# A gated delta-rule layer with a mixture of experts: reciprocal deviations reach all partitions through DRAM instead of through TensorE

## The reference

```python
def step(S, t):
    q_t, k_t, v_t, a_t, b_t = t
    y = einsum('bhvk,bhk->bhv', S, k_t)
    err = y - v_t
    S = a_t[..., None] * S - (b_t[..., None] * err)[..., None] * k_t[:, :, None, :]
    o = einsum('bhvk,bhk->bhv', S, q_t)
    return (S, o)
...
mu = mean(o, axis=-1, keepdims=True)          # over the 128 channels of a head
var = mean(square(o - mu), axis=-1, keepdims=True)
o = (o - mu) * rsqrt(var + LN_EPS) * ln_g + ln_b
o = (o * sigmoid(x @ Wg).reshape(b, t, H, D)).reshape(b, t, H * D)
return o @ Wo
```

## Time and profile before

| what | value |
|---|---|
| median of 3 runs | 3097.45 us (3096.15 to 3103.75) |
| span of the profiled execution | 3102.6 us |
| PE busy | 2732.2 us (88%) |
| DVE busy | 2239.8 us (72%) |
| ACT busy | 1610.3 us (52%) |
| POOL busy | 1377.8 us (44%) |
| granted TensorE clock, mean | 0.976 of full speed |
| DMA queue of SP | 258.51 MB, 31.5% of 16 engines' span |

### The profile page before, as it was taken

One profiled execution on the slowest core, in us unless ns is written; L12 is line 12 of the kernel. 1 busy time (PEld: TensorE's weight loads), 2 busy tenths in 40 slices (PEclk: granted clock), 3 DMA queues, 4 the chain that ended last, 5 costly groups with the idle time before them and its releaser, 6 DMA issues. The chain is left out here.

```text
span 3102.6 us, 48417 instructions
## 1 busy us (share of the span) xinstructions
PE 2732.2 (88%) x14144; PEld 1863.5 (60%) x14144; DVE 2239.8 (72%) x4680; ACT 1610.3 (52%) x3516; POOL 1377.8 (44%) x1760
## 2 busy tenths in 40 slices
PE   7999999768898888988889888898888888859999
PEld 3555555446666666666666666666666666635555
DVE  6777777677888878888788887888887888623332
ACT  6666666545555555555555555555555555412111
POOL 3666676734544445444454444544445444310000
PEclk9999999989999999999999999999999999979999
DMA  3655556533232232322323223232223222034120
GB/s 124 241 225 206 233 230 239 196 82 67 43 57 42 44 65 47 57 42 43 64 49 57 42 44 59 53 57 42 44 51 61 46 53 43 9 107 109 45 38 14
DMA packets 449883, 261.22 MB, mean 84 GB/s; under 512 B 402672, under 2 KB 414672, under 8 KB 447472
## 3 DMA queue, kind: packets, MB, share of 16 engines
q1 hardware_dynamic: 449664, 258.51, 31.5%
HBM read 153.42 MB, written 105.05 MB: 83 GB/s over the span
## 5 line engine op out<-in xcount | busy, mean ns | idle before, releaser
L265 DVE SCALAR_TENSOR_TENSOR A_acc<-A_psY,A_w,A_acc 128x410 f32<-128x410 f32 (+1 forms) x720 | 419.2, 637 | 151.6 <-ACT A_acc L334 151.6
L405 PE MATMUL A_psY<-A_xT,A_w 128*128 128x413 f32 (+1 forms) x960 | 347.2, 510 | 9.1 <-PE A_psAG L411 7.7
L1244 ACT ACTIVATE B_PQ<-B_psM 128x64 f32<-128x64 f32 (+2 forms) x480 | 125.2, 261 | 441.2 <-DVE B_NC L1137 440.9
L1137 DVE TENSOR_TENSOR B_NC<-B_NC,B_psM 128x256 f32<-128x256 f32 x480 | 200.8, 418 | 182.5 <-PE B_psM L1756 92.8
L192 POOL TENSOR_TENSOR A_outs<-A_outs,A_acc 128x410 f32<-128x410 f32 (+1 forms) x240 | 229.7, 987 | 216.1 <-ACT A_outs L342 216.1
L899 POOL TENSOR_TENSOR B_WT<-B_WT,B_G 128x128 f32<-128x128 f32 (+2 forms) x224 | 143.4, 640 | 371.2 <-ACT B_WT L1244 184.3
L1244 ACT ACTIVATE B_WL<-B_psT 64x128 f32<-64x128 f32 (+3 forms) x480 | 148.5, 309 | 265.6 <-PE B_psT L1723 265.4
L405 PEld LDWEIGHTS A_psY<-A_xT,A_w 128*128 128x128 f32 x960 | 180.2, 189 | 165.5 <-issue 164.2
L1140 DVE TENSOR_REDUCE B_W<-B_NC 128x64 f32<-128x320 f32 x512 | 248.7, 486 | 17.6
L334 ACT ACTIVATE A_acc<-A_psY,A_w 128x410 f32<-128x410 f32 (+1 forms) x240 | 166.1, 692 | 162.9 <-PE A_psY L405 161.2
L879 POOL TENSOR_TENSOR B_PQ<-B_PQ,B_G 128x256 f32<-128x256 f32 x128 | 89.4, 699 | 345.5 <-DVE B_WT L1105 345.5
(11 more groups left out here) (207 smaller groups left out, 6588.4 us busy)
## 6 DMA issues: line engine op xcount, KB each, us to landing
B_KQ<-scr SPq DMA_DIRECT2D x96, 512.0 KB, 6.6
scr<-A_outs SPq DMA_DIRECT2D x48, 615.0 KB, 3.5
scr<-A_outag SPq DMA_DIRECT2D x32, 615.0 KB, 5.2
scr<-A_outs SPq DMA_DIRECT2D x48, 409.0 KB, 2.5
A_xc<-nbeta SPq DMA_DIRECT2D x16, 1024.0 KB, 5.9
B_A<-scr SPq DMA_DIRECT2D x32, 512.0 KB, 4.6
B_C<-scr SPq DMA_DIRECT2D x32, 512.0 KB, 6.3
B_G<-scr SPq DMA_DIRECT2D x32, 512.0 KB, 4.6
```

Source lines behind the costliest of these rows:

```text
L265: nc.vector.scalar_tensor_tensor(a, y, w[:, s, col:col + 1], a, ALU.mult, ALU.add)\
L405: last = nc.tensor.matmul(psY[p][:, y0:y0 + HALO + t1 - t0], wp[:, p, kt, :], xT[:, kt, t0:t1 + HALO], start=kt == 0, stop=kt == KT - 1)
L1137: tt(eq[:, :, :, 1:5], eq[:, :, :, 1:5], left.unsqueeze(2).to_broadcast([128, H, R, R]), ALU.mult)\
L1244: copy = lambda out, in_: nc.scalar.activation(out, in_, ACT.Copy)
```

## The change

The variances and the square root stay as they are, but the root moves on ACT from leaf 12 to leaf 11, ahead of `pairs_copy`. The reciprocal is taken of the 8 by 128 tile `sdev` in place, and moves on DVE from leaf 13 to leaf 12. SP then stores the 8 rows (4 KB) to a DRAM tensor `rstd`, waits until the store has landed, and loads them back broadcast to 128 partitions, 4 KB each, into the tile of `SQ`. `norm` reads that tile instead of two PSUM banks. The nine transposes of a chunk and their three jobs go, so the banks are handed out anew. POOL's `decayed_q` waits for `norm` of the chunk before instead of for its root. In `project_inputs` three semaphores per slot, which said that PE, DVE and ACT are done with the weights, become one that each raises by one.

```diff
-        12: ([("gram", 0)] if not last else []) + ([("dev", 0)] if out else []) + ([("wo_rest", 0)] if wo else []),
+        12: ([("gram", 0)] if not last else []) + ([("wo_rest", 0)] if wo else []),
         13: [("decay", 2), ("decay", 3)],
-        14: [("ktok", 1)] + ([("rstd", 0)] if out else []) + ([("wo_rest", 1)] if wo else []) + ([("rstd", 1)] if out else []),
+        14: [("ktok", 1)] + ([("wo_rest", 1)] if wo else []),
...
+            def spread_rstd(o):
+                wait(sp, rd, o, 1)
+                wait(sp, rld, o, 0)
+                sp.dma_start(rstd_d, sdev[:]).then_inc(rst.sem, 16)
+                wait(sp, rst, o, 1)
+                sp.dma_start(FQ, rstd_d.rearrange("i x -> (i x)").partition_broadcast(128)).then_inc(rld.sem, 16)
...
+                if g:
+                    spread_rstd(g - 1)
                 if g % 2 and g >= 3:
                     store((g - 3) // 2)
...
-                wait(pool, sd, o - 1, 1)
+                wait(pool, on, o - 1, 2)
...
             def invert(o):
-                ps = take_bank(dve, o + 1, "dev", 0)
-                nc.vector.reciprocal(rdev[:], ps[:, 0:8]).then_inc(rd.sem, 1)
+                wait(dve, sd, o, 1)
+                nc.vector.reciprocal(sdev[:], sdev[:]).then_inc(rd.sem, 1)
 
             def norm(o, i):
-                ps = take_bank(dve, o + 1, "rstd", i)
+                wait(dve, rld, o, 1)
                 x = O[:, 8 * i:8 * (i + 1), :]
-                tt(x, x, ps[:].rearrange("p (h c) -> p h c", h=8), ALU.mult).then_inc(on.sem, 1)
+                tt(x, x, SQ[:, 8 * i:8 * (i + 1), :], ALU.mult).then_inc(on.sem, 1)
...
                     elif j == 12:
+                        if g:
+                            invert(g - 1)
                         if more:
                             leaf_solution(nxt, 2)
                     elif j == 13:
-                        if g:
-                            invert(g - 1)
...
             def deviation(o):
                 ps = take_bank(act, o + 1, "var", 0)
-                wait(act, rd, o - 1, 1)
+                wait(act, rst, o, 0)
                 nc.scalar.activation(sdev[:], ps[0:8, 0:128], ACT.Sqrt, bias=eps[0:8, 0:1]).then_inc(sd.sem, 1)
...
                     elif j == 11:
+                        if g:
+                            deviation(g - 1)
                         if more:
                             pairs_copy(nxt)
...
                     elif j == 12:
                         if more:
                             block_keys(nxt)
-                        if g:
-                            deviation(g - 1)
```

More of the change, by code:

```diff
@@ L103, in project_inputs @@
         w_ld = [Count(sem(f"A_w_ld{s}"), 1, 16) for s in range(2)]
-        w_used = [Count(sem(f"A_w_used{s}"), 1, 1, 1) for s in range(2)]
-        c_used = [Count(sem(f"A_c_used{s}"), 1, 1, 1) for s in range(2)]
-        ca_used = [Count(sem(f"A_ca_used{s}"), 1, 1, 1) for s in range(2)]
+        w_used = [Count(sem(f"A_w_used{s}"), 3) for s in range(2)]
         y_full = [Count(sem(f"A_y_full{p}"), 2 * NTA) for p in range(3)]
@@ L160, in heads @@
                                  .partition_broadcast(128)).then_inc(bt_ld[s].sem, 16)
-                    sp.wait_ge(w_used[s].sem, w_used[s].at(t, 1))
-                    sp.wait_ge(c_used[s].sem, c_used[s].at(t, 1))
-                    sp.wait_ge(ca_used[s].sem, ca_used[s].at(t, 1))
+                    sp.wait_ge(w_used[s].sem, w_used[s].at(t, 3))
                     sp.dma_start(w[:, s, :], wpack_d[bass.ds(t * 2 + (s + 2), 1)].rearrange("o p c -> p (o c)"))\
@@ L246, in _ @@
                 tap[p].start(dve)
-            c_used[0].start(dve)
-            c_used[1].start(dve)
             with dve.Fori(0, TURNS) as t:
@@ L268, in _ @@
                     dve.wait_ge(tap[2].sem, tap[2].at(t, 3 * (s + 1) * NTA))
-                    dve.sem_inc(c_used[s].sem, 1)
+                    dve.sem_inc(w_used[s].sem, 1)
         @block.scalar
@@ L315, in _ @@
             nc.scalar.activation(nbeta[:], beta[:], ACT.Copy, scale=-SCALE * SCALE).then_inc(nbeta_sb, 1)
-            for c in (*ag_free, *ca_used):
+            for c in ag_free:
                 c.start(act)
@@ L355, in _ @@
                     act.wait_ge(ag_free[0].sem, ag_free[0].at(t, (s + 1) * NTA))
-                    act.sem_inc(ca_used[s].sem, 1)
+                    act.sem_inc(w_used[s].sem, 1)
         @block.tensor
@@ L390, in _ @@
             pe.wait_ge(beta_sb, T // 512)
-            w_used[0].start(pe)
-            w_used[1].start(pe)
             with pe.Fori(0, TURNS) as t:
@@ L460, in chunk_jobs @@
     if g == NCH:
-        return [("qk", n, l) for n in range(3) for l in range(2)] + [("oc", 0), ("oc", 1), ("var", 0), ("dev", 0), ("rstd", 0), ("rstd", 1)]
+        return [("qk", n, l) for n in range(3) for l in range(2)] + [("oc", 0), ("oc", 1), ("var", 0)]
     if g > NCH:
@@ L517, in recurrence @@
         sem = lambda name: ctx.enter_context(nc.semaphore("B_" + name))
+        rstd_d = nc.dram_tensor("rstd", (8, 128), FP32).ap()
         wo = sb("wo", [128, H, HID])
@@ L553, in recurrence @@
         O, SQ = sb("O", [128, H, C]), sb("SQ", [128, H, C])
-        sdev, rdev = spare[0][0:8, 0:128], sb("rdev", [128, 8])
+        sdev = spare[0][0:8, 0:128]
         avgcol = sb("avgcol", [128, 15])
@@ L618, in recurrence @@
         sd, rd, on = Count(sem("sdev"), 1), Count(sem("rdev"), 1), Count(sem("o_normed"), 2)
+        rst, rld = Count(sem("rstd_st"), 1, 16), Count(sem("rstd_ld"), 1, 16)
         aff, nlg, og = Count(sem("o_affine"), 1), Count(sem("negative_gain"), 1), Count(sem("o_gated"), 4)
@@ L649, in taken @@
                     "update": (stu, g, n + 1), "oc": (oc, g - 1, n + 1),
-                    "var": (sd, g - 1, 1), "dev": (rd, g - 1, 1), "rstd": (on, g - 1, n + 1)}[kind],
+                    "var": (sd, g - 1, 1)}[kind],
         def open_bank(pe, *job):
@@ L752, in _ @@
             load("G", 0, T - C)
+            spread_rstd(NCH - 1)
             store(NCH // 2 - 1)
@@ L757, in _ @@
                 loaded(sp, what, NCH - 1)
+            wait(sp, rst, NCH, 0)
+            wait(sp, rld, NCH, 0)
             wait(sp, ldc, NCH, 0)
@@ L1613, in shared_job @@
                                   start=i == 0, stop=i == 7)
[L1614 to L1622, removed]
                 elif kind == "wo":
```

## The result

The changed kernel takes 3148.48 us (median of 4 runs, 3146.71 to 3159.58) against 3098.11 us for the kernel before on the same chip. The ratio is 1.0167, with a 95% interval from 1.0146 to 1.0187: slower by 50 us, where 8 were forecast. The profiled execution has a span of 3145.0 us (3102.6 before) and a mean granted TensorE clock of 0.957 (0.976 before).

What follows compares the result with a forecast made beforehand. Bound: the chunk period, changing hands between the leaf chain, PE in odd chunks and ACT's `WE` copy, plus the tail. Even chunks 13.2 and 2.5 us more, odd 12.0 less, tail 4.6 more: 8.3 over 3097.45, 3106 us; range 3090 to 3125.

Steps and rivals of the forecast that it cites:

- signs of error: Wrong if the odd period does not fall, the even one does not grow, or the reciprocal is over 0.35 us.
- The direction: Whole kernel: 8.3 us more forecast; chances faster 0.13, same 0.42, slower 0.45.
- the stall: ACT's early root delays `pairs_copy` by 2.0 us; leaf 12's first product moves 1.3 us; 1.2 even, 0.5 or 0.6 odd.
- the price of the reciprocal: DVE, 8 by 128: 0.30 us from a product's 1.0 ns an element; hidden in a 0.33 us wait at even leaf 13.
- five even chunks would lose only 0.5 us: Chunks 1, 6, 10, 14 and 30, where DVE waited 0.67 us for the old root-spreading transpose: 2.5 us in all.
- A transpose taken from PE is worth something only in odd chunks: PE at the odd chunk's end: removal lets the `WE` transposes start 0.9 us earlier, about 0.8 us gained.
- gives nothing: Even chunk's end: removing the eight transposes neither gains nor costs, as PE waits 0.61 us for the `WE` copy.
- Rival A: Reciprocal takes 0.89 us: 0.56 more per even chunk, up to 0.7 per odd; 19 us more, 3125; chance 0.13.
- rival D: Clock: moved work may end or start half-rate matmul spells, 10 us either way, 3096 or 3116; chance 0.14.
- Store, load and tail: Load lands in 4.7 us, transfers cost nothing inside the stage; tail 4.6 us later, 2.8 to 6.5 by bounds.
- A product of two SBUF tiles ... no change: `norm` on DVE: 690 ns from two SBUF tiles, 0.69 us with one PSUM operand, so no change.
- The forecast's 8.3: Sum over even chunks, odd chunks and tail: 8.3 us more, to 3106 us; chance 0.52.

Runs made afterwards that it cites:

- e2: The kernel before with only the root moved ahead of `pairs_copy` at leaf 11; 3135.06 us, ratio 1.0108.
- e5: The changed kernel with eight transposes that nobody reads put on PE behind leaf 14's `ktok`, in every chunk from 1 on; 3134.44 us, ratio 1.0109.
- e1: The changed kernel with only the root moved back, behind the copy to `WL` of leaf 11; 3117.34 us, ratio 1.006.
- e6: The changed kernel with late root, reciprocal cut to 8 by 8 (result incomplete) and eight dummy transposes in even chunks only; 3089.45 us, ratio 0.9972.
- e4: The changed kernel with the root behind leaf 11's `WL` copy and the reciprocal cut to 8 by 8 (result incomplete); 3109.25 us, ratio 1.0035.
- e7: The changed kernel with the root behind leaf 11's `WL` copy, full reciprocal and eight dummy transposes in even chunks only; 3098.59 us, ratio 0.9999.
- e3: The changed kernel with the reciprocal cut from 8 by 128 to 8 by 8 elements (result incomplete); 3138.45 us, ratio 1.0123.
- e17: Kernel before, its odd chunks as changed but root behind leaf 11's `WL` copy and `norm` at the end of DVE's chunk; 3108.73 us, ratio 1.0019.

## Why the prediction was wrong

It named as signs of error an odd period that does not fall and a reciprocal over 0.35 us. The odd period fell by 0.09 where 0.8 was forecast, and the reciprocal took 0.93.

The direction and the stall were right. That the removal costs nothing in even chunks, the price of the reciprocal and that of the clock were not.

- The stall was right: 1.89 us of wait at DVE, 1.2 us in an even and 0.5 us in an odd chunk at full clock (e2). That five even chunks would lose only 0.5 us is not settled: 6, 10 and 14 are 1.5 to 2.2 us longer in e2, but with 3.4 to 6.8 us more at the low clock.
- "A transpose taken from PE is worth something only in odd chunks": right for odd ones, 0.83 us (e5 to after), and 1.0 us with the root late (e1 against before). For even ones, "gives nothing" is the step that failed most: 1.51 us each are lost (e5 to after), 22.6 us over 15 chunks, because the transposes filled PE's wait for `WE` and so kept its clock up (2.3 us at 0.50 per even chunk with dummies in e6, 6.1 without in e4; 2.5 in e7, 5.5 in e1). This is an upper value, since in e5 the first product of even chunks is also 0.7 us shorter. With dummies in even chunks alone the medians give 19 to 20 us, 1.3 each (e7 to e1, e6 to e4).
- The reciprocal was the term mis-sized: 0.93 us, not 0.30. Rival A's slope of two rows gave 0.89; from 8 to 128 elements it is (933 - 183) / 120, 6.3 ns an element, against 5.8 between the earlier trace rows's two. That these lie so close is in part luck: e3's 8 elements from SBUF take 183 ns, only 5 more than the earlier trace rows's four, and the line through 183 and 933 would give 158 for four. A had the length of the instruction, 0.89 us, but too much of it on the path: 0.46 of the odd chunk's gain goes and 0.28 us in an even one (e3), where A had up to 0.7 and 0.56. My 1.0 ns an element came from a product, where the measured slope is 6.3, and that step made the error.
- The clock was rival D, at 10 us either way. The spells at 0.50 went from 41 to 150 us over chunks 2 to 30. D priced moved work and left out that removed work and stalls both leave PE idle, 1.48 us ahead of e4's `WE` transposes and 1.66 us (0.89 before) ahead of leaf 12's in the changed kernel.
- Store, load and tail were right: the load lands in 3.5 us (4.7 assumed), hides in the stage, and in the tail `norm` starts 5.7 us after the root ends where 1.9 stood, 3.8 us later against 4.6 forecast. "A product of two SBUF tiles ... no change" was wrong beside POOL: 796 ns on average where 678 stood.

The forecast's 8.3, A's 19 and the 22.6 of even chunks make the measured 50, but this is in part luck: e3 has 10 us for the reciprocal where A has 19, and e2 has 35 us for the root alone. Single changes to the changed kernel give back 31 us for the root, 14 with the dummies and 10 for the reciprocal in medians (33, 18 and 14 by the ratios), more than 50 together: they overlap, through the clock among other things. How long a spell follows from a given idle time is open.

## What to carry over

Before PE work is taken out, look at what PE does in that place: if it stands ahead of a wait, the matmuls behind it may come at half rate (1.94 us for 1.06 here, at a grant of 0.50), so count the removal as a cost and test it with dummies in its place. Do not give an unseen shape the slope of another operation: the reciprocal took 6.3 ns an element from 8 to 128 where 1.0 was carried over from a product, and the slope of its own rows, 5.8, came nearer. When a DVE operand moves from PSUM to SBUF (`norm` went from 678 ns to between 678 and 1290 on average), look at what POOL does at that time, and place the operation where POOL is done.

## What the runs showed of the hardware

- Mean time of a reciprocal from SBUF: 183 ns for 8 by 8, 933 ns for 8 by 128.
- Eight 128 by 128 transposes take 1.04 to 1.06 us at a grant of 1.00 and 1.94 at 0.50, 32 update matmuls 2.06 at 1.00 and 3.79 at 0.50 (e4, chunk 2).
- POOL slows beside DVE too: in e17 its last product took 0.85 us in chunk 8 and 1.29 in chunk 9, where `norm` runs beside it.
